# Expert loops that run over the lot's number, from one expert's first lot to the next one's

## What is computed

```python
x = x + attention(layernorm(x))             # 16 heads of 8 features
# the expert layer, on tgt = layernorm(x):
logits = jnp.einsum('bsd,ed->bse', tgt, Wr) + br         # 8 experts
top_v, top_i = jax.lax.top_k(logits, 2)
top_w = jax.nn.softmax(top_v, axis=-1)
h = jax.nn.relu(jnp.einsum('bsd,efd->bsef', tgt, W1) + b1)   # 512 hidden features
o = jnp.einsum('bsef,edf->bsed', h, W2) + b2
tgt2 = jnp.einsum('bsed,bse->bsd', o, router_w)          # only the two best experts count
x = x + layernorm(tgt + tgt2) * gamma + beta
```

## The kernel before

| | 0 | 1 | 2 | 3 | 4 | 5 | 6 | 7 |
|---|---|---|---|---|---|---|---|---|
| lots in the loop | 2 | 2 | 2 | 2 | 3 | 2 | 2 | 2 |
| TensorE | 39 | 41 | 42 | 44 | 46 | 48 | 49 | 51 |
| VectorE | 32 | 34 | 35 | 37 | 39 | 41 | 43 | 45 |
| ScalarE | 13 | 15 | 16 | 18 | 20 | 22 | 23 | 26 |
| GpSimd | 15 | 17 | 18 | 20 | 22 | 24 | 26 | 28 |

## Time and profile before

### The profile page before, as it was taken

How to read it: one execution, slowest core, us unless ns; L and a number is a source line. 1 busy time by engine, 2 the same in 40 slices (tenths; PEclk the granted TensorE clock), 3 DMA queues, 4 the chain that set the end, 5 groups by cost and what they waited for, 6 DMA issues and landing times.

```text
span 648.4 us, 12762 instructions
## 1 busy us (share of the span) xinstructions
PE 591.1 (91%) x3656; PEld 320.6 (49%) x3656; DVE 486.0 (75%) x1287; ACT 436.7 (67%) x886; POOL 232.9 (36%) x397
## 2 busy tenths in 40 slices
PE   2889999999999999999999999999899999998872
PEld 1634333433343433343334343333399989988730
DVE  3577898999899999899899898896155444444358
ACT  2634788788788788888888877778664444443323
POOL 8110010022331422512512331231477775454445
PEclk9965999999999999999999999999999999999986
DMA  6751812212303302411331231113105222222172
GB/s 202 250 159 46 189 39 74 76 48 83 104 27 96 112 27 75 118 40 44 100 89 30 86 97 51 31 34 98 54 31 151 83 81 71 62 70 65 32 275 114
DMA packets 46622, 56.98 MB, mean 88 GB/s; under 512 B 8366, under 2 KB 25818, under 8 KB 46564
## 3 DMA queue, kind: packets, MB, share of 16 engines
q1 hardware_dynamic: 40580, 45.06, 24.3%
q0 software_dynamic: 4544, 8.53, 3.9%
q10 hardware_dynamic: 1440, 2.69, 1.2%
HBM read 29.28 MB, written 27.16 MB: 87 GB/s over the span
## 4 chain that ended last, share of the span: by engine, by line
PE 60%; DVE 20%; ACT 8%; issue 5%; POOL 3%; DMA 2%; DVEq 0%; SPq 0%; ACTq 0%; POOLq 0%
PE pv_psum L1063 12%; DVE mneg L770 10%; PE st_psum L993 10%; PE s_psum L977 10%; PE y_psum L1554 6%; ACT pt L651 4%; PE y_psum L1230 3%; PE side_psum L1025 2%; PE side_psum L999 2%; PE h_psum L1545 2%; PE side_psum L1019 2%; ACT xn L669 2%; PE h_psum L1547 2%; PE h_psum L1546 2%; DVE split L777 2%
## 5 line engine op out<-in xcount | busy, mean ns | idle before, releaser
L770 DVE TENSOR_REDUCE mneg<-s_psum 128x1 f32<-128x512 f32 x512 | 323.0, 684 | 31.6 <-PE s_psum L977 30.1
L651 ACT ACTIVATE pt<-st_psum 128x512 f32<-128x512 f32 x512 | 279.2, 598 | 68.3 <-PE st_psum L993 63.6
L977 PE MATMUL s_psum<-ks,qs 64*128 64x512 f32 x512 | 204.0, 472 | 3.0 <-DVE mneg L770 1.9
L993 PE MATMUL st_psum<-qs,ks 64*128 64x512 f32 x512 | 194.2, 458 | 8.1 <-ACT pt L651 7.7
L977 PEld LDWEIGHTS s_psum<-ks,qs 64*128 64x128 f32 x512 | 83.2, 190 | 108.8 <-DVE mneg L770 87.0
L1063 PE MATMUL pv_psum<-pt,vst 128*16 128x512 f32 x1024 | 134.5, 598 | 0.0
L993 PEld LDWEIGHTS st_psum<-qs,ks 64*128 64x128 f32 x512 | 79.8, 187 | 52.4 <-ACT pt L651 41.4
L1420 ACT ACTIVATE hid<-h_psum,b1c 128x384 f32<-128x384 f32 x68 | 36.9, 582 | 53.8 <-PE h_psum L1547 53.8
L1386 POOL DMA_INDIRECT results<-res,goal_now x51 | 49.9, 979 | 42.5 <-DVE res L1468 28.5
L510 POOL DMA_INDIRECT sent<-xrow,placeu x56 | 54.5, 974 | 16.2 <-issue 16.2
L1554 PE MATMUL y_psum<-w2t,hid 128*128 128x128 f32 x408 | 48.7, 275 | 1.2 <-DVE ysum L1462 1.2
(11 more groups left out here) (219 smaller groups left out, 803.2 us busy)
## 6 DMA issues: line engine op xcount, KB each, us to landing
parts<-split SPq DMA_DIRECT2D x48, 256.0 KB, 3.0
ks<-parts SPq DMA_DIRECT2D x128, 48.0 KB
qs<-parts SPq DMA_DIRECT2D x128, 48.0 KB
lot<-sent SPq DMA_DIRECT2D x18, 198.0 KB
sent<-tail SPq DMA_DIRECT2D x16, 198.0 KB, 5.0
xres<-in_L_attn_x_dram SPq DMA_DIRECT2D x8, 256.0 KB, 3.2
pt<-in_L_ffn_W_dram SPq DMA_DIRECT2D x1, 2048.0 KB, 14.1
got<-results SPq DMA_DIRECT2D x8, 256.0 KB, 6.3
```

What stands on the lines that cost most here:

```text
L651: nc.scalar.activation(pt[:, n % PT_SLOTS, (g + 2) % 4, :], st_psum[:, k % ST_BANKS, :], ACT.Exp, scale=SCALE).then_inc(exp_done, 1)
L770: nc.vector.tensor_reduce(mneg[:, (n // 4) % 2, at:at + 1], s_psum[:, k % S_BANKS, :], AX_X, ALU.max, negate=True).then_inc(max_done, 1)
L977: mm(s_psum[:, k % S_BANKS, :], qs[rows, c, P * (n % 4):P * (n % 4) + P], ks[rows, c, g, :], start=True, stop=True).then_inc(s_made, 1)
L993: mm(st_psum[:, k % ST_BANKS, :], ks[rows, c, g, P * (n % 4):P * (n % 4) + P], qs[rows, c, :], start=True, stop=True).then_inc(st_made, 1)
```

## The change

In the loops of GpSimd, ScalarE, VectorE and TensorE the counter itself is the lot's number: it runs from `first[e]` to `first[e + 1]`, where it ran from 0 to `turns[e]` and `first[e]` was added in the body. The bodies use u as before. SyncE's loops are as they were.

```diff
 # GpSimd; the same edit in scalar (act), vector (dve) and tensor (pe)
         for e in range(E):
             if e % (E // 2) == 0:
                 early.stored(pool, e // (E // 2))
-            with pool.Fori(0, turns[e]) as i:
-                u = first[e] + i
+            with pool.Fori(first[e], first[e + 1]) as u:
                 for h in range(HALVES):
                     pool.wait_ge(y_done, (u * HALVES + h + 1) * 2)
...
-            with act.Fori(0, turns[e]) as i:
-                u = first[e] + i
+            with act.Fori(first[e], first[e + 1]) as u:
...
-            with dve.Fori(0, turns[e]) as i:
-                u = first[e] + i
+            with dve.Fori(first[e], first[e + 1]) as u:
...
-            with pe.Fori(0, turns[e]) as i:
-                u = first[e] + i
+            with pe.Fori(first[e], first[e + 1]) as u:
```

## The result

The first comparison gave 643.30, 650.93, 651.79 and 640.12 us for the changed kernel (median of all four 647.12), 648.87, 650.49, 650.55 and 659.05 us for the kernel before, and a ratio of 0.9872, 95% interval 0.9834 to 0.9910. The change makes the kernel faster by 1.3%; 643.5 us had been forecast.

What follows compares the result with a forecast made beforehand. TensorE bounds the loops, its sequencer reworking the sum before each lot. Twelve distances at 5.13 (61.56) plus entries 0.75 and turns back 0.14 make 62.45 for 69.32 us: gain 6.9, forecast 643.5 us, range 641.9 to 647.2.

Steps and rivals of the forecast that it cites:

- What bounds the loops: Loops: TensorE is the path, busy 69.42 of 74.69 us; its sequencer reworks the sum before a lot's first matmul.
- The straight line: TensorE's loops: lot distance grows 0.12 us per body instruction, from 5.13 us near 41 instructions.
- The Trainium skill's queue: TensorE's loop heads: by the 64-deep queue alone, queued W2 matmuls would cover the head and the gain be 0.
- rival 2: TensorE's loops: no change, 650.5 us; the idle is something else and the queue covers register work; chance 0.07.
- Ends: Loop ends: one addition more, about 40 instructions a body; a turn back costs 5.13 us plus 0.02, at most 0.07.
- rival 1: Loop ends and entries: the register isn't reused, so the sum moves and doubles; 5.5 us slower, 656 us; chance 0.08.
- Between experts: TensorE's entries into an expert's loop: 45 instructions on the path, 0.15 us each, with 0.07 and 0.21 as ends.
- Edits at nothing: Heads of VectorE, ScalarE and GpSimd, SyncE's waits: shorter heads or earlier goals lie within other waiting; gain 0.
- The sum: Lot 4's start to lot 16's: 69.32 us becomes 62.45, gain 6.9 us, between 6.2 and 7.8.
- What is late next: Loops after the change: TensorE itself limits at 5.13 us a lot; the tightest other ring has 0.7 us of room.
- The scatters' ring: VectorE's third part and GpSimd's scatters: 5.52 us needed against 6.2 us, so 0.7 us of room.
- Rival 3: TensorE's loops: a 1.6 us stall, as on GpSimd, hits one expert's two lots, giving back 3.2: 646.7 us; chance 0.10.

Runs made afterwards that it cites:

- pe_only: The change made in TensorE's loops alone, the other three engines as in the kernel before: 642.31 us, ratio 0.9882 to the kernel before.
- pe_not: The change made in GpSimd, ScalarE and VectorE, TensorE as in the kernel before: 648.31 us, ratio 0.9988 to the kernel before.
- hoist: The kernel before, its loops from 0 kept, with first[e] moved into a register ahead of each of the four engines' loops: 642.13 us, ratio 0.9873.
- pe_mid12: The changed kernel with 12 useless register instructions mid-body on TensorE, between the turning and the W2 matmuls: 638.24 us, one run.
- before_y3: The kernel before, sums in the bodies, with an own PSUM bank for W2's third part in the loops, removing its wait: 641.0 us, ratio 0.9873.
- pe_head12: The changed kernel with 12 useless register instructions at the head of each TensorE loop body: 659.72 us, one run.
- after_y3_head12: The changed kernel with an own PSUM bank for W2's third part and 12 useless register instructions at TensorE's body heads: 645.62 us, one run.
- pe_dose: The changed kernel with 2 x e useless register instructions at the head of expert e's TensorE body: 651.72 us, one run.

## Why the prediction was right, point by point

*What bounds the loops.* Right, and shown: TensorE, and in it the idle before a lot's first matmul (`pe_only`, `pe_not`); by the place of the sum (`hoist`). I called it the sequencer working the sum out ahead of the first matmul; the runs add what I had not seen, that this work is late because it stands behind the third part's wait (`pe_mid12`, `before_y3`). I had counted a body's instructions and taken 41 as what a lot's time covers; 52 are covered when 12 of them stand ahead of that wait. The straight line held all the same, since the sums grew only at the head.

*The Trainium skill's queue* ("Advanced Engine Details and Errata", sections "Sequencer Loop" and "Engine Queue Depths") stood beside rival 2: engine instructions are queued, 64 deep on TensorE, and others are read meanwhile. In the kernel before that doesn't cover the head; without the third part's wait it nearly does, with 12 more instructions at 0.14 us a lot where they cost 1.1. So the runs agree with the rule where no such wait lies ahead, and show the wait that ended it here. What inside TensorE is held by a wait on a matmul these runs don't show.

*Ends.* Right: one addition more, 40 instructions, and turns back at 5.11 to 5.17 us. `first[e]`'s register is used again, as SyncE's `skip` had suggested; rival 1 did not come.

*Between experts.* Too dear: 0.15 us each had been taken from lots 4 and 6, with 0.07 as the lower end; lots 6, 8, 11, 13 and 15 take 5.13 to 5.19, 0.04 over on average. In the compiled program the addition and the move became one instruction, so that the path has 44 instructions and not 45 (43 into lot 11, which takes 5.13), and for 44 the rows had said 0.07. The upper end had been read too low: from start to start lot 6 took 546.97 - 541.50 = 5.47, not 5.34, since the chain begins an overlapped matmul late.

*Edits at nothing.* Right: `pe_not`, which has the other engines' shorter heads alone, gains nothing from lot 4 to lot 16. Lots 0 to 3 stayed within the 0.4 allowed: into lot 3 it takes 6.74 us, 6.90 before.

*The sum.* 62.45 us from lot 4 to lot 16 were forecast, 61.76 came: the gain of 6.9 was 7.6 by the chain, near the upper end of 7.8. That the profiled execution took 643.3 us, almost the 643.5 forecast, is partly luck: it lost 0.7 us ahead of lot 4. By the repeated runs, 641.3 us, the forecast was 2.2 us too slow, and they lie 0.6 us below its range; the mis-sized entries explain 0.5 of it, and the rest is within the spread of the runs.

*What is late next.* Right: TensorE is busy in 66.94 of 66.94 us from lot 3's start on. The scatters' ring and the lot's load show up singly where VectorE's heads stay long (`pe_only`, `before_y3`).

*Rival 2*, that "issue" is something else, falls with `pe_head12`: the same instructions, put back without the sum, bring the idle back. *Rival 3*: GpSimd's stall stayed on GpSimd, 1.86 us.

## What to carry to other kernels

Count the register instructions between an engine's last real wait in a loop body and the first instruction of the next turn: here those were late, at 0.10 us each on TensorE beyond what was covered, and an expression that looks computed once may be computed in every turn. Either work the value out ahead of the loop, in straight code, or move that last wait earlier; each of the two brought the whole gain here, and both together no more than the runs can tell from one. Idle time put down to "issue" that grows from one copy of a loop to the next is worth reading beside the compiled instruction counts.

## What the runs showed of the hardware that was not expected

Here a wait in TensorE's program decided what register work was covered, more than the work's amount: 12 instructions cost nothing ahead of the W2 stage's waits and 1.1 us a lot behind them. And most of the spread between the traced runs lies ahead of the loops: from lot 4's start to lot 16's, five of the seven with short lots take 61.5 to 61.9 us, `pe_only` and `before_y3`, where a lot was late, 62.2 and 62.6, while over all twelve traces lot 0's first matmul stands between 509.77 us (`pe_mid12`) and 514.88 (`after_y3_head12`). The granted clock of the whole execution goes with it: 0.978 in `pe_mid12`, 0.974 in `pe_not` (511.41) and `pe_dose` (511.65), and 0.966 to 0.970 in the nine whose lot 0 starts at 513.45 or later.
